# Splitting the normalised rows into fp16 halves before the transpose instead of after it

## The reference, cut to what matters

```
x = x + 0.5 * ffn(layernorm(x))
x = x + ssm(layernorm(x))
x = x + 0.5 * ffn(layernorm(x))
# ffn: e = argmax(x @ Wr) of 8 experts, p = its softmax probability
#      out = p * (gelu(x @ W1[e] + b1[e]) @ W2[e] + b2[e]),   W1[e]: 256x1024, W2[e]: 1024x256
```

## Time and profile before

| | us |
|---|---|
| median of 3 runs | 669.21 (660.31 to 678.82) |
| the profiled execution's own time | 666.62 |
| its span, first to last instruction | 664.8 |
| PE busy | 567.4 (85%) |
| DVE busy | 480.9 (72%) |
| ACT busy | 415.9 (63%) |
| POOL busy | 264.7 (40%) |

### The profile page before, as it was taken

How to read it: one execution, slowest core, us unless ns; L and a number is a source line. 1 busy time by engine, 2 the same in 40 slices (tenths; PEclk the granted TensorE clock), 3 DMA queues, 4 the chain that set the end, 5 groups by cost and what they waited for, 6 DMA issues and landing times.

```text
span 664.8 us, 18534 instructions
## 1 busy us (share of the span) xinstructions
PE 567.4 (85%) x6466; PEld 515.4 (78%) x6466; DVE 480.9 (72%) x1027; ACT 415.9 (63%) x963; POOL 264.7 (40%) x258
## 2 busy tenths in 40 slices
PE   6980139999999999999979884489889999999996
PEld 5980039899998898999957563388778999999996
DVE  6759966677887886777469999355646777677774
ACT  3897966666666666666246643266547667667663
POOL 0040182455555455452121104624554555555522
PEclk9555559999999999999988997589999999999999
DMA  8997030111111111111232321301111111111210
GB/s 273 368 377 265 13 95 27 50 44 46 46 48 43 43 49 48 43 43 27 71 135 84 100 73 64 109 25 34 43 41 42 49 47 49 48 45 50 48 32 1
DMA packets 31800, 52.12 MB, mean 78 GB/s; under 512 B 6747, under 2 KB 23837, under 8 KB 31456
## 3 DMA queue, kind: packets, MB, share of 16 engines
q1 hardware_dynamic: 21728, 32.03, 14.0%
q0 software_dynamic: 9984, 18.93, 10.4%
HBM read 38.08 MB, written 14.71 MB: 79 GB/s over the span
## 4 chain that ended last, share of the span: by engine, by line
PE 74%; DVE 12%; issue 7%; DMA 3%; ACT 2%; SPq 1%; ACTq 0%; POOL 0%; POOLq 0%; DVEq 0%
PE banks L1127 33%; PE banks L1144 10%; PE banks L1145 10%; PE banks L1146 10%; PE banks L1039 3%; PE banks L1103 3%; DVE weights_arena L608 2%; DMA weights_arena<-L_attn_u 2%; PE banks L1033 1%; DVE weights_arena L962 1%; DVE weights_arena L982 1%; DVE weights_arena L972 1%; DVE weights_arena L1003 1%; PE banks L1202 1%; PE banks L1196 1%
## 5 line engine op out<-in xcount | busy, mean ns | idle before, releaser
L520 ACT ACTIVATE weights_arena<-banks,b1t,inv 128x128 f32<-128x128 f32 x624 | 227.5, 469 | 76.7 <-PE banks L1127 61.3
L1127 PE MATMUL banks<-weights_arena 128*128 128x128 f16 x3744 | 234.4, 222 | 10.6 <-issue 6.5
L1127 PEld LDWEIGHTS banks<-weights_arena 128*128 x3744 | 221.7, 99 | 19.3 <-issue 16.6
L1145 PE MATMUL banks<-weights_arena 128*128 x624 | 170.0, 273 | 1.6 <-issue 1.3
L1144 PE MATMUL banks<-weights_arena 128*128 x624 | 170.1, 273 | 1.4 <-issue 1.0
L1146 PE MATMUL banks<-weights_arena 128*128 x624 | 170.1, 273 | 0.5 <-issue 0.3
L832 DVE TENSOR_SCALAR weights_arena<-weights_arena,hscale 128x512 f16<-128x512 f32 x156 | 77.1, 494 | 83.8 <-ACT weights_arena L520 83.1
L835 DVE SCALAR_TENSOR_TENSOR weights_arena<-weights_arena,hscale 128x512 f16<-128x512 f32 x156 | 117.2, 751 | 5.6
L386 POOL DMA_INDIRECT recf<-records,sorti x78 | 79.0, 1013 | 24.0 <-issue 24.0
L502 ACT ACTIVATE weights_arena<-banks,xscale 128x256 f16<-128x256 f32 x78 | 37.1, 476 | 82.1 <-PE banks L1103 62.4
L395 POOL DMA_INDIRECT out<-weights_arena,sorti x39 | 39.8, 1020 | 104.5 <-DVE weights_arena L851 94.0
(11 more groups left out here) (197 smaller groups left out, 595.5 us busy)
## 6 DMA issues: line engine op xcount, KB each, us to landing
weights_arena<-L_ffn_W SPq DMA_DIRECT2D x16, 1024.0 KB, 12.6
weights_arena<-x_after_ffn SPq DMA_DIRECT2D x8, 528.0 KB, 4.3
weights_arena<-L_attn_u SPq DMA_DIRECT2D x8, 512.0 KB, 10.0
x_after_ssm<-weights_arena SPq DMA_DIRECT2D x8, 512.0 KB, 2.9
weights_arena<-L_ffn_b SPq DMA_DIRECT2D x2, 1024.0 KB, 5.0
recf<-records,sorti POOLq DMA_INDIRECT x78
weights_arena<-L_attn_u,sorti POOLq DMA_INDIRECT x39
x_after_ffn<-weights_arena,sorti POOLq DMA_INDIRECT x39
```

Of the source, the lines that this page charges most:

```text
L520: last = act.activation(hb[q % 2][:, f, :], src, ACT.Gelu, bias=b1t[:, bass.ds(e * FC + f, 1)], scale=inv1[:, bass.ds(e, 1)])
L1127: last = pe.matmul(acc[:, f * P:(f + 1) * P], weights[wpart * DC + d], xts[q % 2][:, xpart, d, :], start=(n == 0), stop=(n == 5))
L1145: pe.matmul(acc, hs[q % 2][:, 0, f, :], low, start=False, stop=False)
```

## The change

The normalised rows are split while tokens are still in partitions, ahead of the transpose, with the constant factor SX = 2^10. ACT writes the high half right after `norm`, DVE the low half (`split_rows`), into a new buffer `halves` (two of them). PE transposes four 128x128 fp16 blocks instead of two float32 ones, into the first half of the same PSUM bank read as fp16. DVE `copy_x` reads all 512 fp16 numbers of the bank in one instruction, multiplies by the expert's factor (which no longer holds SX) and writes both parts of `xts`. ACT no longer reads the bank. ACT prepares three tiles ahead instead of two for `norm` and one for `high_x`, and loads the expert's number just ahead of gelu. A fp16 identity is made at the start; an integer helper array moves to another place in memory.

```
 # ACT
                 def norm(q):
                     if q >= 2:
-                        act.wait_ge(s["turned"], q - 1)
+                        act.wait_ge(s["rows"], q - 1)
...
                 def high_x(q):
-                    e = experts[q] = act.value_load(eid[0:1, q:q + 1], min_val=0, max_val=E - 1)
-                    act.wait_ge(s["turned"], q + 1)
+                    norm(q)
                     if q >= 2:
-                        act.wait_ge(s["m1"], q * 2 - 2)
-                    act.activation(xts[q % 2][:, 0], bank[6 + q % 2][:, 0:DC * P]..., ACT.Copy,
-                                   scale=xscale[:, bass.ds(e, 1)]).then_inc(s["xt_hi"], 1)
-                norm(0)
-                norm(1)
-                high_x(0)
+                        act.wait_ge(s["turned"], q - 1)
+                    act.wait_ge(s["xn"], 2 * q + 1)
+                    act.activation(halves[q % 2][:, 0, :], xng[q % 2], ACT.Copy, scale=SX).then_inc(s["xn"], 1)
+                for q in range(3):
+                    high_x(q)
                 for q in range(NT):
-                    if q + 2 < NT:
-                        norm(q + 2)
-                    if q + 1 < NT:
-                        high_x(q + 1)
-                    e = experts[q]
+                    if q + 3 < NT:
+                        high_x(q + 3)
+                    e = act.value_load(eid[0:1, q:q + 1], min_val=0, max_val=E - 1)
 # DVE
+            dve.tensor_scalar(ident_h[:], iota_r[:], part[:], None, ALU.is_equal)
...
-                def split_x(q):
+                def split_rows(q):
+                    dve.wait_ge(s["xn"], 2 * q + 2)
+                    dve.scalar_tensor_tensor(halves[q % 2][:, 1, :], xng[q % 2], SX, halves[q % 2][:, 0, :], ALU.mult,
+                                             ALU.subtract).then_inc(s["rows"], 1)
+                def copy_x(q):
                     e = experts[q] = dve.value_load(eid[0:1, q:q + 1], min_val=0, max_val=E - 1)
-                    dve.wait_ge(s["xt_hi"], q + 1)
-                    dve.scalar_tensor_tensor(xts[q % 2][:, 1], src, sc, xts[q % 2][:, 0], ALU.mult, ALU.subtract) \
-                        .then_inc(s["xt"], 1)
+                    dve.wait_ge(s["turned"], q + 1)
+                    if q >= 2:
+                        dve.wait_ge(s["m1"], q * 2 - 2)
+                    dve.tensor_scalar(xts[q % 2], turned_x(q), xscale[:, bass.ds(e, 1)], None, ALU.mult).then_inc(s["xt"], 1)
...
-                split_x(0)
-                split_x(1)
+                split_rows(0)
+                split_rows(1)
+                copy_x(0)
+                copy_x(1)
+                split_rows(2)
                 split_h(0)
                 for q in range(NT):
                     if q + 2 < NT:
-                        split_x(q + 2)
+                        copy_x(q + 2)
+                    if q + 3 < NT:
+                        split_rows(q + 3)
                     if q + 1 < NT:
                         split_h(q + 1)
                     result(q)
 # PE
                 def turn_tile(q):
-                    pe.wait_ge(s["xn"], q + 1)
+                    pe.wait_ge(s["rows"], q + 1)
                     if q >= 2:
                         pe.wait_ge(s["xt"], q - 1)
-                    for d in range(DC):
-                        last = pe.transpose(bank[6 + q % 2][:, d * P:(d + 1) * P], xng[q % 2][:, d * P:(d + 1) * P],
-                                            ident[:])
+                    for half in range(2):
+                        for d in range(DC):
+                            last = pe.transpose(turned_x(q)[:, half, d, :], halves[q % 2][:, half, d * P:(d + 1) * P], ident_h[:])
                     last.then_inc(s["turned"], 1)
```

More of the change, by code:

```diff
@@ L98, in macaron @@
         part_i = sb("part_i", [P, 1], I32)
-        iota_i = sb("iota_i", [P, P], I32)
         ident = sb("ident", [P, P])
+        ident_h = sb("ident_h", [P, P], F16)
         upto = sb("upto", [P, P], BF16)
@@ L184, in macaron @@
         xng = [view(9728 + k * D, D) for k in range(2)]
+        halves = [view(10752 + k * D, 2, D, dt=F16) for k in range(2)]
         xts = [view(10240 + k * 256, 2, DC, P, dt=F16) for k in range(2)]
@@ L248, in macaron @@
                 "diff exps onehot counts rec_ready rec_stored pos row rowused sorted_sb owned b2in xn turned "
-                "xt_hi xt m1 gelu h_hi hsplit m2 o_chain o").split()}
+                "rows xt m1 gelu h_hi hsplit m2 o_chain o").split()}
             S[ph]["gath"] = [sem(f"gath{k}_{ph}") for k in range(RING)]
@@ L264, in in_slot, with turned_x @@
             return len(range(k, NT, RING))
+        def turned_x(q):
+            return bank[6 + q % 2][:, 0:D].bitcast(F16).rearrange("p (h c t) -> p h c t", h=2, c=DC)
         def loads(n):
@@ L285, in macaron @@
         namef = view(15104, 2, 2, NJ)
+        iota_i = view(15232, P, dt=I32)
         braw = view(14336, D)
@@ L356, in _ @@
             chain = Chain(pool, pool_chain)
-            pool.iota(iota_i[:], [[1, P]], base=0, channel_multiplier=0).then_inc(iota_done, 1)
+            pool.iota(iota_i, [[1, P]], base=0, channel_multiplier=0).then_inc(iota_done, 1)
             pool.iota(part_i[:], [[0, 1]], base=0, channel_multiplier=1).then_inc(iota_done, 1)
@@ L492, in norm @@
                                    scale=recf[:, q % RING, 1:2]).then_inc(s["xn"], 1)
-                experts = {}
                 def high_x(q):
-                    e = experts[q] = act.value_load(eid[0:1, q:q + 1], min_val=0, max_val=E - 1)
-                    act.wait_ge(s["turned"], q + 1)
+                    norm(q)
                     if q >= 2:
-                        act.wait_ge(s["m1"], q * 2 - 2)
-                    act.activation(xts[q % 2][:, 0], bank[6 + q % 2][:, 0:DC * P].rearrange("p (c t) -> p c t", c=DC), ACT.Copy,
-                                   scale=xscale[:, bass.ds(e, 1)]).then_inc(s["xt_hi"], 1)
-                norm(0)
-                norm(1)
-                high_x(0)
-                for q in range(NT):
-                    if q + 2 < NT:
-                        norm(q + 2)
-                    if q + 1 < NT:
-                        high_x(q + 1)
-                    e = experts[q]
+                        act.wait_ge(s["turned"], q - 1)
[3 more added lines that the diff above has]
+                    high_x(q)
+                for q in range(NT):
+                    if q + 3 < NT:
+                        high_x(q + 3)
+                    e = act.value_load(eid[0:1, q:q + 1], min_val=0, max_val=E - 1)
                     for half in range(2):
@@ L562, in _ @@
             dve.wait_ge(iota_done, 2)
-            dve.tensor_copy(iota_r[:], iota_i[:])
+            dve.tensor_copy(iota_r[:], iota_i)
             link(dve.tensor_copy(part[:], part_i[:]))
@@ L679, in product_scales @@
                 link(dve.reciprocal(gall[:], gall[:]))
-                link(dve.scalar_tensor_tensor(xscale[:], of(wmag, 0), SX, of(gall, 0), ALU.mult, ALU.mult))
+                link(dve.scalar_tensor_tensor(xscale[:], of(wmag, 0), 1.0, of(gall, 0), ALU.mult, ALU.mult))
                 dve.scalar_tensor_tensor(hscale[:], of(wmag, 1), TOP, of(gall, 1), ALU.mult, ALU.mult)
@@ L813, in ffn @@
                 experts = {}
-                def split_x(q):
-                    e = experts[q] = dve.value_load(eid[0:1, q:q + 1], min_val=0, max_val=E - 1)
-                    src = bank[6 + q % 2][:, 0:DC * P].rearrange("p (c t) -> p c t", c=DC)
-                    sc = xscale[:, bass.ds(e, 1)]
-                    dve.wait_ge(s["xt_hi"], q + 1)
-                    dve.scalar_tensor_tensor(xts[q % 2][:, 1], src, sc, xts[q % 2][:, 0], ALU.mult, ALU.subtract) \
-                        .then_inc(s["xt"], 1)
+                def split_rows(q):
[3 more added lines that the diff above has]
+                def copy_x(q):
+                    e = experts[q] = dve.value_load(eid[0:1, q:q + 1], min_val=0, max_val=E - 1)
+                    dve.wait_ge(s["turned"], q + 1)
+                    if q >= 2:
+                        dve.wait_ge(s["m1"], q * 2 - 2)
+                    dve.tensor_scalar(xts[q % 2], turned_x(q), xscale[:, bass.ds(e, 1)], None, ALU.mult).then_inc(s["xt"], 1)
                 def split_h(q):
```

## The result

The changed kernel takes 722.45 us (median of 4 runs, 718.98 to 725.7). The kernel before, with a fourth run added, has a median of 665.51 us. The ratio is 1.092 (95% interval 1.087 to 1.097): 57 us slower, where 675 us, a range of 661 to 688 and "within 2%" at 0.68 were predicted. A ratio here leaves out the executions that fell in a slower state of the chip, so it can differ a little from the ratio of the medians.

The account below looks back on a forecast made before the run. The prediction took PE's queue as the bound, with DVE the bound in phase 1's nine `double` steps. It summed 666.6 + 5.2 (DVE in `double` steps) + 1.2 (DVE lag afterwards) + 1.8 (starts) = 674.8, so 675 us, range 661 to 688.

Parts of the forecast that it names:

- The step that failed: ACT's look-ahead: gathers wanted a step earlier but issued six tiles ahead, so priced at nothing.
- DVE's cost: DVE's `split_rows` and `copy_x` replacing L821: net +0.50 us a step (0.34 to 0.78), unhidden in nine `double` steps.
- The kernel before in its `double` steps: Phase 1 before the change: DVE is the bound for nine steps and PE follows, 5.73 us each over seven.
- Starts: Entry and phase starts: +1.2 us in phase 1, +0.4 in phase 2, 0.2 for the fp16 identity; sum 1.8.
- Rival five: PE: fp16 transposes cost 0.11 us each, 78 x 0.22 = 17 us, giving 692 us; chance 0.05.
- The slower one: `turn_tile`: its new wait bites in every disturbed pair, 10 to 15.6 us more, giving 687 us; chance 0.15.
- The faster rival: Both phases: looking ahead three tiles removes the disturbed pairs, giving 661 us, or 656 with DVE's cost absorbed; chance 0.12.

Follow-up runs that it names:

- 1, a_look2: Changed kernel with ACT preparing two tiles ahead instead of three: 699.5 us, ratio 1.019 to the kernel before.
- 2, a_ring7: Changed kernel with a ring of 7 gathered tiles instead of 6, three tiles ahead kept: 677.3 us, ratio 0.987 to the kernel before.
- 4: Kernel before with a ring of 5 gathered tiles instead of 6, nothing of the change in it: 707.9 us, ratio 1.032.
- 3, a_fetch_first: Changed kernel with POOL issuing the gather of tile q + 6 ahead of the scatter of tile q: 684.0 us, ratio 0.990.
- 10, a_result_first: Changed kernel with only DVE's order turned, result(q) ahead of split_h(q + 1): 679.9 us, ratio 1.056 to the kernel before.
- b_ring7: Kernel before with a ring of 7 gathered tiles instead of 6: 643.7 us, ratio 0.997.
- a_ring7_again: Changed kernel with a ring of 7 instead of 6, on the same chip as the kernel before with that ring: 649.0 us, ratio 1.003.
- experiments 5 and 6: Kernel before and changed kernel, each with a ring of 7 instead of 6, on one chip: 643.7 us and 649.0 us, ratios 0.997 and 1.003.
- Experiment 8: Changed kernel looking two tiles ahead, with phase 2's scatter cut from 128 to 8 rows a tile but the first: 658.4 us, ratio 1.017.

## Why the prediction was wrong

**The step that failed** is in the part on ACT: "The gathers are wanted a step earlier; they are issued six tiles ahead, so I price this at nothing too." They are six tiles ahead in number, not in time. POOL may fetch tile q + 6 only after `result(q)` has freed the buffer. What had to be priced is the ring: gather, `norm`, the gelu queued behind it, `split_h`, `result`, scatter, next gather. It takes 13.25 us in the round shown. Ring size minus look-ahead minus one tile for DVE's order is the number of tiles over which it is spread: 6 - 2 - 1 = 3 before, 4.4 us each, 1.1 under PE's step; 6 - 3 - 1 = 2 after, 6.6 us each, 1.1 above it. The price is 76 steps by some 0.7 us, the 50.5 us found. Five runs move this pace, by four different terms, and their steps go with it: look-ahead (1, in phase 1 only), ring (2, and 4 in the kernel without the change), the length of the round (3), DVE's order (10, in full only in phase 2).

The prediction did name `norm` as waiting with "the gelu of the tile in hand queued behind". It priced that wait by the gaps of 0.79 and 1.18 us, which are the gaps of a queue whose gathers come in time.

**DVE's cost.** Right in mechanism and near in size. Net +0.50 us a step was taken. In the `double` steps DVE's step grew from 41.05 / 7 = 5.86 us (b_ring7) to 44.06 / 7 = 6.29 (a_ring7_again), +0.43. `copy_x` was taken "near L832" and took 0.484 us for 512 numbers, as long as L821 took for 256 float32 numbers from PSUM. The Trainium skill ("VectorE: DVE Perf Modes", on why PSUM operands drop a tier) allows two elements per cycle for 16-bit PSUM reads and one for float32, and this trace agrees: 0.484 us, against 0.752 us for the two-input L841 on 512. In the changed kernel this cost was mostly hidden under the round. The 5.3 us between experiments 5 and 6 are the size of the change once the ring is gone, where 8.2 had been predicted.

**The kernel before in its `double` steps.** The prediction read 5.73 us of PE a step as PE following DVE. b_ring7 has PE at 5.52 up to 197.19 us with DVE at 5.86: PE's queue lives on its lead nearly to the end. In the execution of before too, `product1` starts 0.22 us after the transposes in all of these steps but the last, at 204.77, so the gap that the prediction showed stands for that one step only. With ring 7, on another chip, phase 1 has 5.45 us a step against 5.67, so a part of the excess was most likely the irregular steps of that execution, not DVE.

**Starts.** In phase 1, from the last weight split's start to `product1`: 95.69 - 92.39 = 3.30 us before, 99.99 - 95.47 = 4.52 after, +1.22 against 1.2 predicted. In phase 2, from the first `norm` to `product1`: 427.79 - 424.43 = 3.36 before, 463.22 - 459.51 = 3.71 after, +0.35 against 0.4.

**fp16 transposes.** Rival five is out: `product1` follows them by 0.22 us in a_result_first's even steps (530.05 to 530.27), as after the float32 ones.

**The rivals.** The slower one was right in sign and put the new wait in `turn_tile`. PE does wait there (34.9 us), but as a consequence: with ring 7 the same wait is, apart from the starts of the phases, 0.21 to 0.86 us in four of the `double` steps. The faster rival, that looking ahead by three tiles would take the irregular pairs away, did not come true for a ring of 6: the third tile of look-ahead is what costs, and pairs such as 9.51 and 4.44 us still stand near the end of phase 2.

**Left open.** What makes the irregular long and short steps. They were there in the first profile of the kernel before, in a_look2 and, milder (4.8 and 6.3 to 6.9 us, one step of 7.6), in a_ring7. They were not in a_fetch_first on the same chip, nor in any ring-7 kernel on chips 13 and 9. Experiment 8 was to tell and could not. The records narrow it down to PE: idle time inside `product1` that ended with nothing named is 6.5 us in 17 gaps before, 16.6 in 48 in a_look2, 14.2 in 36 in a_ring7 and 10.6 in 36 in a_fetch_first, and at most 0.8 us in every profile of chips 13 and 9. So it goes with the chip or the execution rather than with the ring, and some orders absorb it better than others. What holds PE there is not shown.

## What to carry to other kernels

When a consumer is moved earlier in its queue, follow the buffer, not the index: who frees it, what that release waits for, and whether the work queued behind the consumer is part of that wait. The length of that round divided by the tiles it spans is a second pace beside the busiest engine's, and it is a matter of whole tiles: here one step of look-ahead took a third of the span away and one more buffer gave it back. A wait list without waits for the gather says only that the round is shorter than the step, not by how much. And a long wait in the list need not cost anything: in experiment 10 `norm` still waited 113 us.

## What the runs showed of the hardware

From the start of an indirect gather's issue to the start of the ACT instruction that waited for it passed 2.4 and 2.8 us in the rows shown (540.29 to 542.71, 553.20 to 555.96), and 2.3 to 4.3 us over the 67 waits of the changed kernel. In the rows shown each issue holds POOL for 0.97 to 1.21 us with 0.3 between two. Three of them in a row, with the landing, take 5.55 of the 13.25 us (550.41 to 555.96). The same kernel differs much between measurements: the kernel before had medians of 665.5, 689.2, 646.6 and 647.1 us, the last three on chips 14, 13 and 9, while the kernel bound by the round had 722.5 and 719.7.
